# A fused attention-and-experts layer on one core: GpSimd's three scatters of a step set apart, two of them behind signals of TensorE

## What is computed

```python
x = L0_attn_x
xn = _layernorm(x, axis=-1)
x = x + attn(xn) + experts(xn)

# attn: q, k, v, g = xn@Wq, xn@Wk, xn@Wv, xn@Wg ; gk = log_sigmoid(xn@Wgk + bgk) / 16
#       A = (q k^T) * exp(decay differences), lower triangle only
#       o = A v + (decayed q) S ; S = decayed S + (decayed k)^T v
on = o * jax.lax.rsqrt(jnp.mean(o * o, axis=-1, keepdims=True) + EPS) * gnorm_w
out_attn = (on * (g * jax.nn.sigmoid(g))) @ Wo

# experts: expert_idx = argmax(softmax(xn @ gate_w)); expert_w its probability
for e in range(NUM_EXPERTS):
    h = jax.nn.gelu(x_flat @ w1[e] + b1[e], approximate=False)
    y = h @ w2[e] + b2[e]
    out = out + jnp.where(expert_idx == e, expert_w, 0.0)[:, None] * y
```

## Time and profile before

| | us |
|---|---|
| median of 3 runs | 447.07 (446.12 to 447.21) |
| the profiled execution, device time | 444.98 |
| its span, first to last instruction | 443.3 |
| granted TensorE clock over the span | 0.988 of full speed |

### The profile page before, as it was taken

One profiled execution on the slowest core, in us unless ns is written; L12 is line 12 of the kernel. 1 busy time (PEld: TensorE's weight loads), 2 busy tenths in 40 slices (PEclk: granted clock), 3 DMA queues, 4 the chain that ended last, 5 costly groups with the idle time before them and its releaser, 6 DMA issues.

```text
span 443.3 us, 12400 instructions
## 1 busy us (share of the span) xinstructions
PE 419.6 (95%) x3074; PEld 366.9 (83%) x3075; DVE 308.5 (70%) x930; ACT 310.6 (70%) x952; POOL 287.4 (65%) x245
## 2 busy tenths in 40 slices
PE   8997999999999999999999999989999999999990
PEld 6665788888778877877877888889999999999990
DVE  5985798897756757657667567866766776866760
ACT  3688888687867867767678678746666766666660
POOL 8530253456776776767767763417888888888884
PEclk9999899999999999999999999999999999999996
DMA  9725378336456343454454444004554555555540
GB/s 239 190 83 170 140 235 302 139 116 163 134 145 175 91 130 114 120 154 154 134 160 134 117 132 134 12 29 72 70 68 63 71 62 65 69 66 64 74 37 0
DMA packets 59096, 51.29 MB, mean 116 GB/s; under 512 B 7200, under 2 KB 51392, under 8 KB 59072
## 3 DMA queue, kind: packets, MB, share of 16 engines
q1 hardware_dynamic: 45936, 42.07, 34.0%
q0 software_dynamic: 12272, 8.54, 14.0%
q10 hardware_dynamic: 864, 0.40, 0.4%
HBM read 33.14 MB, written 18.30 MB: 116 GB/s over the span
## 4 chain that ended last, share of the span: by engine, by line
PE 63%; ACT 14%; POOL 5%; issue 5%; another core or an unknown queue 5%; DVE 4%; ACTq 1%; DVEq 0%; POOLq 0%
PE psA L905 14%; PE psVG L893 14%; ACT E L1069 8%; PE psO L746 7%; PE psVG L716 5%; POOL rms L544 4%; PE psA L729 4%; PE psQK L704 3%; PE psO L631 2%; PE psO L759 2%; DVE ms L1384 2%; PE psT L770 2%; PE psT L778 2%; ACT sq L1078 2%
## 5 line engine op out<-in xcount | busy, mean ns | idle before, releaser
L578 POOL DMA_INDIRECT out_dram<-yw,sidx x71 | 114.9, 1618 | 29.0 <-issue 9.1
L544 POOL TENSOR_TENSOR rms<-msn,neg_half 128x8 f32<-128x8 f32 x32 | 53.2, 1661 | 42.8 <-DVE msn L1388 42.8
L1069 ACT ACTIVATE E<-gcB,ngc 128x128 f32<-128x128 f32 x256 | 78.5, 400 | 0.0
L746 PEld LDWEIGHTS psO<-v_sb,pr 128*128 128x128 f32 x512 | 64.6, 191 | 14.7 <-issue 12.0
L746 PE MATMUL psO<-v_sb,pr 128*128 128x64 f32 x512 | 66.5, 273 | 8.5 <-DVE og L1428 4.7
L550 POOL DMA_INDIRECT sorted_rows<-x_all,pos_i x64 | 63.3, 989 | 17.1 <-issue 17.1
L537 POOL TENSOR_SCALAR_AFFINE_SELECT E<-E 128x1024 f32<-128x1024 f32 x32 | 35.5, 1111 | 51.5 <-ACT E L1069 51.0
L1384 DVE TENSOR_REDUCE ms<-sq 128x8 f32<-128x512 f32 x32 | 21.9, 686 | 62.1 <-ACT sq L1078 62.0
L1078 ACT ACTIVATE sq<-psO 128x512 f32<-128x512 f32 x32 | 19.1, 596 | 41.9 <-remote 40.0
L1416 DVE TENSOR_TENSOR pr<-psA,E 128x512 f32<-128x512 f32 x64 | 40.9, 680 | 0.0
L905 PE MATMUL psA<-xT_all,v_sb 128*128 x288 | 38.2, 276 | 0.4 <-issue 0.4
(11 more groups left out here) (191 smaller groups left out, 957.2 us busy)
## 6 DMA issues: line engine op xcount, KB each, us to landing
gcB<-decay_rows SPq DMA_DIRECT2D x32, 512.0 KB
sorted_rows<-blank SPq DMA_DIRECT2D x12, 396.0 KB, 5.6
xg<-sorted_rows SPq DMA_DIRECT2D x71, 66.0 KB
x_all<-in_L_attn_x_dram SPq DMA_DIRECT2D x16, 256.0 KB, 5.3
out_dram<-res SPq DMA_DIRECT2D x32, 128.0 KB
eqB<-decay_exp_rows SPq DMA_DIRECT2D x32, 64.0 KB
w1b<-in_L_ffn_w_dram SPq DMA_DIRECT2D x8, 256.0 KB
xT_all<-in_L_ffn_w_dram SPq DMA_DIRECT2D x32, 64.0 KB
```

Source lines behind the costliest of these rows:

```text
L544: nc.gpsimd.tensor_tensor(rms[:], msn[:], neg_half[:, 0:2 * H], ALU.pow).then_inc(rms_ready, 1)
L578: nc.gpsimd.indirect_dma_start(out=out_rows, out_offset=bass.IndirectOffsetOnAxis(ap=sidx[j][:], axis=0), in_=yw[j][:], in_offset=None, bo ...
L746: last = nc.tensor.matmul(psO[:, k * HV + h * DV:k * HV + (h + 1) * DV], pr[:, h // 2, k * SEQ + h % 2 * P:k * SEQ + (h % 2 + 1) * P], v_s ...
L1069: last = nc.scalar.activation(E[j][:, k, h * P:(h + 1) * P], gcB[j][:, k * H + h, :], ACT.Exp, bias=ngcf[:, bass.ds((s * 2 + k) * H + h, 1)])
```

## The change

GpSimd's list of a step is written in another order. Before: mask, power, three scatters. After: mask, a wait for `qk_ready` of the next sequence, one scatter, power, one scatter, a wait for `oT_ps_ready` of the previous sequence, one scatter. The 64 scatters, their data and their steps stay (three in each of steps 7 to 27, one in step 28). The other engines' lists do not change.

```diff
-            def place_rows(s):
-                pool.sem_inc(tick, 1)
-                for t in range(s * 3, min(s * 3 + 3, TILES)):
+            def place_rows(t):
+                if t < TILES:
+                    pool.sem_inc(tick, 1)
                     nc.gpsimd.indirect_dma_start(out=sorted_dram, ...).then_inc(placed, 16)

             def step(s):
+                t = (s - PLACE_FROM) * 3
                 if s < SEQS:
                     mask_dec(*divmod(s, 2))
+                if s == PLACE_FROM:
+                    pool.wait_ge(dve_late, LATE)
+                    pool.wait_ge(sort_cleared, CLEARS * 16)
+                if s >= PLACE_FROM and t < TILES:
+                    pool.wait_ge(qk_ready, s + 2)
+                    place_rows(t)
                 if s >= 1:
                     if s >= 2:
                         pool.wait_ge(dve_on, s - 1)
                     rms_step(*divmod(s - 1, 2))
                 if s == 2:
                     finish_band()
-                if s == PLACE_FROM:
-                    pool.wait_ge(dve_late, LATE)
-                    pool.wait_ge(sort_cleared, CLEARS * 16)
-                if s >= PLACE_FROM:
-                    place_rows(s - PLACE_FROM)
+                if s >= PLACE_FROM and t + 1 < TILES:
+                    place_rows(t + 1)
+                    pool.wait_ge(oT_ps_ready, s)
+                    place_rows(t + 2)
```

## The result

| | median, us | |
|---|---|---|
| before, beside the changed kernel | 447.68 (446.12 to 450.85, 16 runs) | |
| after | 444.50 (442.83 to 447.36, 16 runs) | ratio 0.992, 95% interval 0.990 to 0.995 |

What follows compares the result with a forecast made beforehand. It took TensorE's signals, held beside scatters, to stretch steps from 7.40 to 8.06 us. With 7.5 us expected, 22 steps save 12.3 us, from a median of 447.07 to 434.8 us; range 431.5 to 442.

Steps and rivals of the forecast that it cites:

- What bounds, and the hold: TensorE's signals held 1.7 to 2.0 us after a scatter's start, making `sq` late; 14.5 us at stake over 22 steps.
- No change: Rival: cost goes with the number of scatters, 0.22 us each wherever they lie; 447 us, chance 0.06.
- slower: Rival: second scatter holds the transposes' signal, delaying the mask; loop of 8.6 us, 458.5 us, chance 0.14.
- Third scatter and mask: Third scatter and mask between transposes and `pr`: hidden by the projections with 0.3 us to spare, loop of 7.08.
- First scatter: Scatter ahead of the power: makes power and `on` later, but hidden with 0.6 us to spare before the transposes.
- The rival with v and g: First scatter delays the signal for v and g by a full 2.0 us: 7.72 a step, 439.6 us, chance 0.16.
- Second scatter: Scatter right behind the power: its hold delays signals, making a GpSimd loop of 7.4 to 7.7 us a step.
- The rest: Step 7's new wait for `pos_i`, last scatter, SyncE's queue and experts' part: the step 7 wait was put at nothing.
- The sum: 22 steps, each going from 8.06 to 7.5 us, save 12.3 us; median forecast 434.8 us.

Runs made afterwards that it cites:

- e12: Kernel before plus a fill of a spare 128x512 tile between the second and third scatter, on chip 2: 438.32 us against 446.08, ratio 0.983.
- e13: Kernel before with only the third scatter moved behind a wait for the transposes, on chip 2: 445.57 us against 446.08, ratio 1.000.
- e9: Kernel before reordered to mask, third scatter of the step before, power, two scatters, no new wait, on chip 2: 431.44 us against 447.63, ratio 0.964.
- e8: Kernel before with only the first scatter moved ahead of the power, waiting for q and k, on chip 8: 441.54 us against 431.21, ratio 1.022.
- e5: Kernel before, unchanged, profiled on chip 8: 431.58 us against 431.21, ratio 1.000.
- e6: Changed kernel, unchanged, on chip 8: 445.88 us against 431.21 for the kernel before, ratio 1.032.
- e7: Kernel before with only the third scatter moved behind a wait for the transposes, on chip 8: 441.31 us against 431.21, ratio 1.023.
- e2: Changed kernel with the third scatter waiting for the step's outputs instead of the transposes, on chip 12: 439.48 us, ratio 1.020 to the kernel before.
- e1: Changed kernel without the third scatter's wait for the transposes, on chip 12: 440.08 us, ratio 1.022 to the kernel before.
- e3: Changed kernel with the third scatter behind the next step's mask and no wait for the transposes, on chip 12: 438.79 us, ratio 1.019 to the kernel before.
- e14: Mask, third scatter of the step before, power, then an added wait for `on` before two scatters, on chip 2: 440.52 us, ratio 0.988 to the kernel before.

## Why the prediction was right in its cause and wrong in its size

- **What bounds, and the hold**: right for chips of this kind. e12 and e13 show the late signal beside scatters in a row, and with the scatters set apart the wait for "remote" is gone. The 14.5 us at stake are right too: e9's scatter stretch is 183.7 us, 14.8 less than in the first trace, and its median is 16.2 below that of before on such a chip. That they depend on the chip was in no row of one trace.
- **"No change" and "slower"**: the medians exclude the first, by their interval. The second was the right place with the wrong cause: the mask did end up behind the transposes, the loop it put at 8.6 us for a late signal is 7.92 without one. On a chip without the hold the changed kernel is slower, by 14.7 us, though no rival said why.
- **Third scatter and mask: the step that failed.** It promised 0.3 us to spare and a loop of 7.08. Term by term against the timeline above: start behind the transposes 0.2, measured 0.82, so +0.62. Mask to `pr` 0.06, measured 0.15, +0.09. `og` to the outputs 0.07, measured 0.13, +0.06. Outputs to the end of the transposes 2.78, measured 2.87, +0.09. Scatter, mask and `og` were right to 0.02. Together 7.92, 0.52 above the floor of 7.40. The 0.20 to 0.30 of the earlier trace rows are gaps between instructions none of which has a wait that is still open; taking them for the time from a signal to a scatter was the error. A bound from above was missing.
- **First scatter**: "hidden with 0.6 to spare" failed in two terms, which the third scatter's loop covers up in the changed kernel. The scatter was put right behind the mask, at 2.6, and starts 0.82 after the projection of q and k, at 2.9 to 3.0 in e8. And `res` is missing in it: the transposes need `res`, done 1.22 after the start of `on`, and not `on` alone. In e8 they start 0.25 late for it. Its scatter stretch is 9.0 us longer than that of e5, 2.9 of it in the first two steps and 0.3 a step after them. The rival with v and g didn't come: `th` follows the projection (180.20 + 0.39) at once, at 180.75 in the timeline read above; the scatter there is isolated.
- **Second scatter**: the loop of 7.4 to 7.7 through its hold was built on a hold that isolated scatters don't show: beside the other two of after, `th` and `qb` come 0.13 to 0.16 after their signals. The second one itself is no test, for the `sq` that follows it by 1.67 us couldn't have started earlier.
- **The rest**: the first wait in step 7 was put at nothing. In after, as in e6, the steps that begin at step 7 and 8 take 8.17 and 8.93 us, together 1.26 more than two steps of 7.92. The first scatter of all starts 1.09 us after q and k are projected, and so the power, `on` and the transposes of that step are late.
- **The sum**: 22 x (8.06 - 7.92) = 3.1 us, where the forecast had 22 x (8.06 - 7.5). The medians differ by 3.2. That these two agree is in part luck, for the sum leaves out the way in: the two traces have 177.3 and 175.0 us for the same 22 steps, 2.2 less.

## What to carry to other kernels

To put a DMA behind another engine's signal costs more than the wait: here 0.82 us from the signal to the scatter, and all that stands behind it waits as long, even where it has been ready for long. First look for a place in the list where the work fits without a wait, as between the mask and the power (e9: 3.6% faster on the chip with the hold, no different on the other), and before calling time "to spare", read in the program every wait of the instruction that needs it: the 0.6 us ahead of the transposes were counted to `on`, while `res` behind it was the one they waited for. When a profile shows time lost to something that it can't name, run the same kernel on a second chip before building a change on it.

## What the runs showed of the hardware that was not expected

- **Chips differ, for one and the same program**: 446 to 448 us on chip 2 and in the first comparison, 430.5 to 431.2 on chips 8, 12 and 13. The granted clock was no part of it (0.988 in the first trace, 0.985 in e5).
- **From a signal to an indirect DMA that waits for it**: 0.82 us after the transposes (after, e6, e7), the outputs (e2), the projection of q and k (e1, e2, e3, e8) and, at 0.83, `on` (e14), each but for the first step or a stray one. In e3 the scatter ahead of it was still running when the signal came, and it is 0.82 all the same. The mask started 0.18 after the exponentials that it waited for (e3).
- **`msn` and the mask.** An operation on 128x8 elements that takes 0.17 us took 1.80 in after: it started at 178.24, beside a scatter and 0.67 ahead of the mask, and ended at 180.04, 0.03 after the mask. In e8 it started while the mask ran and ended 0.03 after it; GpSimd's row, then VectorE's:

```profile
183.19 1.10 POOL L537 TENSOR_SCALAR_AFFINE_SELECT E<-E 128x1024 f32<-128x1024 f32 x1
```

```profile
183.43 0.89 DVE L1393 SCALAR_TENSOR_TENSOR msn<-ms,vpe 128x8 f32<-128x8 f32 x1
```

  In e3 and e9, where it starts behind the mask, it takes 0.17. The Trainium skill ("SBUF — State Buffer", section "Who interferes with whom") says that a VectorE instruction with two SBUF inputs contends with a GpSimd instruction that reads SBUF; both of `msn`'s inputs lie there. By that rule the mask holds it, and e8's trace agrees. For after the rule is not enough: there `msn` had started first, and what held it until the mask began isn't shown. It costs some 31 us of VectorE's busy time (32 x (1.131 - 0.167)). `pr` starts 0.12 after its end, 0.15 after the mask's; whether a short `msn` would let `pr` start earlier no run shows.
- **`on` and a scatter.** A scatter that starts 0.10 us after `on` takes 1.50 instead of 0.96 us (183.05 in after, 164.10 in e9); one that is 0.58 us under way when `on` starts takes its usual 1.03 (171.36 in e5, `on` at 171.94). So what starts first keeps its pace there. The runs don't tell what they share.
